# Attention and FFN layer: the value products of a group move from two sections of the PE program into one

## The reference, cut to what matters

```
n = layernorm(x)
q, k, v = n @ Wq, n @ Wk, n @ Wv        # 32 query heads, 8 key/value heads, 16 wide; rotary on q and k
att = q k^T / 4, causal                 # 4 query heads share one key/value head
ctx = softmax(att) @ v
x = x + ctx @ Wo
x = x + (silu(layernorm(x) @ Wg.T) * (layernorm(x) @ Wu.T)) @ Wd.T    # 1376 wide
```

## Time and profile before

| | |
|---|---|
| median of three runs | 810.72 us |
| the profiled execution's own time | 811.23 us |
| its span, from the first to the last instruction | 809.5 us |
| granted TensorE clock, mean over the span | 0.983 |
| busy: PE, DVE, ACT, POOL | 776.1, 432.7, 344.5, 210.3 us |

### The profile page before, as it was taken

One profiled execution on the slowest core, in us unless ns is written; L12 is line 12 of the kernel. 1 busy time (PEld: TensorE's weight loads), 2 busy tenths in 40 slices (PEclk: granted clock), 3 DMA queues, 4 the chain that ended last, 5 costly groups with the idle time before them and its releaser, 6 DMA issues.

```text
span 809.5 us, 12354 instructions
## 1 busy us (share of the span) xinstructions
PE 776.1 (96%) x4449; PEld 528.1 (65%) x4480; DVE 432.7 (53%) x744; ACT 344.5 (43%) x684; POOL 210.3 (26%) x382
## 2 busy tenths in 40 slices
PE   5789999999999999899799999999999999999998
PEld 4635555555555554354388887888878888788886
DVE  7686788687876777787345553223323243141112
ACT  3417768666777667667644232111112211121111
POOL 3406764467526863233400000000000000000000
PEclk9959999999999999999999999999999999999999
DMA  7436577234332336462168200512004120020001
GB/s 259 107 89 232 171 248 225 75 100 118 92 96 78 108 93 182 141 189 59 53 202 238 79 27 0 169 41 78 27 1 155 52 78 26 0 104 0 1 1 52
DMA packets 74613, 81.86 MB, mean 101 GB/s; under 512 B 8720, under 2 KB 58384, under 8 KB 74352
## 3 DMA queue, kind: packets, MB, share of 16 engines
q1 hardware_dynamic: 74128, 80.77, 32.8%
q10 hardware_dynamic: 432, 0.39, 0.2%
HBM read 57.02 MB, written 33.36 MB: 112 GB/s over the span
## 4 chain that ended last, share of the span: by engine, by line
PE 50%; DVE 0%; issue 0%; DVEq 0%
PE bank L1476 34%; PE ps_y L1528 15%; PE bank L1515 1%; DVE x_in L1458 0%; DVEq L1457 0%
## 5 line engine op out<-in xcount | busy, mean ns | idle before, releaser
L855 DVE TENSOR_REDUCE m_raw<-ps_s 128x1 f32<-128x512 f32 (+3 forms) x352 | 210.8, 634 | 65.7 <-PE ps_s L1099 63.1
L724 ACT ACTIVATE probs<-ps_t 128x512 f32<-128x512 f32 (+1 forms) x352 | 185.8, 563 | 101.8 <-PE ps_t L1126 100.6
L1433 DVE TENSOR_TENSOR h<-h,bank 128x512 f32<-128x512 f32 (+1 forms) x44 | 30.2, 687 | 216.8 <-PE bank L1476 216.1
L1096 PE MATMUL ps_s<-k_rows,q_rows 96*128 96x256 bf16 (+3 forms) x512 | 134.1, 315 | 7.1 <-DMA q_rows<-scratch_q_parts 4.6
L1126 PE MATMUL ps_t<-q_rows,k_rows 98*128 98x512 bf16 (+1 forms) x352 | 127.5, 367 | 6.5 <-DMA q_rows<-m_t 2.9
L1096 PEld LDWEIGHTS ps_s<-k_rows,q_rows 96*128 96x128 bf16 x512 | 44.2, 99 | 70.7 <-issue 30.5
L1371 ACT ACTIVATE h<-bank 128x512 f32<-128x512 f32 (+1 forms) x44 | 26.3, 599 | 149.1 <-PE bank L1476 149.1
L632 POOL TENSOR_SCALAR_AFFINE_SELECT probs<-probs 128x512 f32<-128x512 f32 x128 | 84.8, 662 | 0.0
L1139 PE MATMUL ps_o<-probs,v_ones 128*32 128x512 f32 (+3 forms) x1024 | 82.4, 440 | 0.3 <-ACT o_sb L734 0.3
L1377 ACT CAST h_hi<-h 128x512 fp32r<-128x512 f32 (+1 forms) x44 | 27.3, 620 | 127.1 <-DVE h L1433 127.1
L217 POOL TENSOR_TENSOR var_eps<-mean_var,eps 128x1 f32<-128x1 f32 x16 | 3.1, 191 | 289.9 <-DVE mean_var L212 289.9
(11 more groups left out here) (150 smaller groups left out, 1343.7 us busy)
## 6 DMA issues: line engine op xcount, KB each, us to landing
scratch_o<-o_sb SPq DMA_DIRECT2D x31, 256.0 KB, 2.3
q_rows<-scratch_q_parts SPq DMA_DIRECT2D x32, 192.0 KB
x_in<-in_x SPq DMA_DIRECT2D x16, 256.0 KB, 5.0
q_rows<-scratch_q_parts SPq DMA_DIRECT2D x32, 128.0 KB
x_res<-in_x SPq DMA_DIRECT2D x16, 256.0 KB, 2.7
o_in<-scratch_o SPq DMA_DIRECT2D x64, 64.0 KB
inverse<-scratch_inverse SPq DMA_DIRECT2D x64, 64.0 KB
out<-x_in SPq DMA_DIRECT2D x16, 256.0 KB, 2.1
```

The costliest lines, as they stand in the source:

```text
L724: nc.scalar.activation(probs[:, g % 2, heads * u:heads * (u + 1), CHUNK_AT[c]:CHUNK_AT[c + 1]], ps_t[:, pos % S_BANKS, 0:heads * CHUNK_N[c ...
L855: nc.vector.tensor_reduce(out=m_raw[:, g % 2, at:at + heads], op=ALU.max, axis=AXIS.X, in_=ps_s[:, (BANK_AT[i] + u) % S_BANKS, 0:heads * w ...
L1096: nc.tensor.matmul(bank[:, place], q_rows[r][0:ROWS, j, P * q:P * (q + 1)], k_rows[r][0:ROWS, 0:width], start=(place == 0), stop=False)
L1433: nc.vector.tensor_tensor(h[0:m, r], h[0:m, r], bank[units["up", f] % BANKS][0:m, :], ALU.mult).then_inc(h_ready, 1)
```

## The change

One entry of `PV_AT` now holds all four chunks, at (1, 1) of the next group, and the entry for (3, 3) is gone. After the last group, which has no next one, four chunks instead of two follow the loop. Nothing else is changed: no wait, no buffer, no DMA and no other engine's program.

```diff
-PV_AT = {(1, 1): (-1, (2, 3)), (3, 3): (0, (0, 1))}
+PV_AT = {(1, 1): (-1, (0, 1, 2, 3))}
 PV_EVACUATE = 2
...
                 if not has_next:
-                    for c in (2, 3):
+                    for c in range(TT):
                         weighted_v(b, NKV - 1, c)
```

## The result

| | before | after |
|---|---|---|
| median of five runs | 810.33 us (808.09 to 813.69) | 829.11 us (828.23 to 830.91) |
| the profiled execution's own time | 811.23 us | 830.91 us |
| its span | 809.5 us | 829.2 us |
| granted TensorE clock, mean | 0.983 | 0.977 |

The ratio is 1.0228, with a 95% interval from 1.0197 to 1.0259: **2.3% slower**, 18.8 us. The forecast was 823.0, from 811 to 830.

The account below looks back on a forecast made before the run. PE was taken to set the time of phase 1, DVE and ACT following with some slack. 811.2 - 6.2 + 12 + 6.5 = 823.5, and with the median 0.5 lower 823.0 us, range 811 to 830.

Parts of the forecast that it names:

- The clock's rival: Longer wait before group 25 brings a second half-clock stretch, 1.7 us, groups 30 and 31 as much again: 826.5; chance 0.09.
- the rival without a merging gain: Entering chunk 2 in the merged section costs a new entry, so the 6.2 us are not saved: 829 us; chance 0.05.
- Part 1: One section less in each of groups 0 to 30: 0.20 us saved on PE, 31 times, 6.2 us.
- Part 2: PE reaches (0, 0) 1.73 us earlier, DVE and ACT come late to a group's first banks: 12 us lost.
- the groups like 12: Groups where the rotated queries' splits end late; group 12 loses about 1.2 us, group 20 about 0.9.
- The POOL collision: A POOL operation stretches DVE's split of the maxima in group 12, 1.01 us against 0.18; 1.6 us taken off.
- the prediction's own sign: If groups without dense pieces or like group 11 are longer too, the forecast's mechanism is wrong.
- 11's pattern: In group 11 ACT is not late and DVE by 0.78 us, with 1.0 spare: nothing is lost.
- the fourth score bank needs the first reduce: At a group's start, this bank's need leaves DVE 1.0 us spare, so lateness below that costs nothing.
- Part 3: SP's staged rows and maxima come late at group starts, PE's way being 1.93 us shorter: 6.5 us lost.
- The rivals of the other side: DVE and ACT absorb their lateness, only DMA bites: 811.0, chance 0.14; or nothing is late, only the saving: 804.5, chance 0.09.

Follow-up runs that it names:

- experiments 2: Kernel after, with chunks 0 and 1 also multiplied a second time, for nothing, at (3, 3): 854.31 us, ratio 1.0567.
- experiments 3: Kernel after, with the merged section split: chunks 0 and 1 at (1, 0), chunks 2 and 3 at (1, 1) of the next group: 830.69 us, ratio 1.025.
- experiment 8: Kernel after, with batch 3's eight loads and the stores of the rotated rows issued behind the maxima's DMA on SP: 822.09 us, ratio 1.0167.
- experiment 1: Kernel before, with the section at (1, 1) in two, chunk 3 going to (1, 2): 817.0 us, ratio 1.0078.
- Experiment 9: Kernel after, with the three score banks used in turn across groups, without a restart at bank 0: 829.07 us, ratio 1.0202.
- experiment 5: Kernel after, with batch 3's eight loads issued one slot later on SP, behind the maxima's DMA: 824.36 us, ratio 1.0189.

## Why the prediction was right, and where it was not

**The sign and the mechanism held; the place within the range is partly luck.** It named DVE, ACT and SP, each late at a group's start once the section at (3, 3) is gone, and that is where the time went: experiments 2 and 3 show that the empty (3, 3) makes the loss, and experiment 8 parts the rows' share from the banks'. But 829.11 is 0.9 us inside the upper bound and 6.1 above the 823.0, and below, errors of 2 us cancel. The clock's rival, 826.5, was nearer, and 829, the number of the rival without a merging gain, is met for another reason.

**Part 1, one section less: 6.2 us, and it is 7.4.** The pieces of the earlier trace rows gave 0.20 a group, experiment 1 measured 0.24 and the kernel after shows 0.23. The rival without a merging gain is out.

**Part 2, DVE and ACT: the size held, the places half.** In the 22 groups without DMA or clock the sum was met (6.4 against 6.3) by luck, with two errors of over 2 us that cancel:
- In the groups like 12 the prediction had some 1.0, 0.8 and 0.7 us for 12, 4 and 20 (after the 0.20); they gave -0.12, 0.03 and 0.31. The POOL collision did not come back there, which the forecast had allowed 1.6 us for. The split of the maxima in group 12, for the 1.01 us of the earlier trace rows:

```profile
195.25 0.18 DVE L864 TENSOR_TENSOR m_parts<-m_raw,m_parts 128x16 bf16<-128x16 f32 x1 [0.59 <-ACT m_parts L705]
```

It moved instead, to groups 1, 9 and 17, where the split took 0.30, 0.24 and 0.24 us before and takes 1.02, 1.01 and 1.02 after. In group 9:

```profile
160.60 1.01 DVE L864 TENSOR_TENSOR m_parts<-m_raw,m_parts 128x16 bf16<-128x16 f32 x1 [1.14 <-ACT m_parts L705]
```

- In the groups that were to lose little or nothing (8, 16, 18, 21, 24: -0.20 to 0.0 each) it was 0.00 to 0.25. By the prediction's own sign, that its mechanism is wrong if the groups without dense pieces or with 11's pattern are longer too, this counts against it: 24, without such pieces, is 0.12 longer, and 3, 11 and 19 come to 0.03 only when SP's order is mended. The sign foretold 0.22 us between the product before (0, 0) and the next, and it is 0.38. The step that failed is "the fourth score bank needs the first reduce ... 1.0 us is spare". At a group's start the restart of the ring asks for more: the first two banks need the last two reduces. Experiment 9 shows that this slack is the tight one there, and that in its trace easing it alone mostly moves the wait.

**Part 3, the rows: right in the sum.** Forecast 6.5; PE's waits for rows and maxima grew by 4.3 + 1.1 = 5.4 us, and by 6.6 with the waits at the starts of groups 11 and 19 (0.65 and 0.53), which the profile puts down to ACT and DVE but SP's order took away. By places it was not met: 3, 7, 11 and 19 wait 0.53 to 0.69 us for 0.6 to 1.3 forecast, and 23, which the forecast didn't have, 0.69. Experiment 8 took most of it away by the order of SP's queue alone (1.1 + 1.5 us are left). The wait ahead of group 25 rose by 1.12 us (2.93 to 4.05) and not by 1.93. SP's chain in the kernel after:

```profile
323.01 0.36 SPq L443 DMA_DIRECT2D scratch_o<-o_sb  x1
...
333.43 0.72 SPq L437 DMA_DIRECT2D q_rows<-m_t  x1
```

It takes 10.4 us to the issue of the maxima, as before (10.5). PE was ready for them 11.24 us after the chain's start before and is after 9.86, so its way is 1.38 shorter and not 1.93: PE loses some 0.55 on it itself, which the forecast gave back in groups 3 to 11 but not here. The other 0.26 is that the maxima were there sooner after the chain's start, 13.91 us for 14.17. Group 5's wait was larger, 2.63 for 0.38 before and 0.9 forecast on top; it was 1.30 in experiments 3 and 5, so it differs between executions.

**The clock: the term that was mis-sized.** The sum had it at nothing, and a rival with 0.09 had 3.4 us of it, one more stretch after the wait ahead of group 25 and as much in groups 30 and 31. Measured are two more behind that wait, one more in 30 and 31, and one in group 5: four of 3.4 us. What one costs shows where a group has the same waits in two traces and the stretch in one of them only: group 31 1.83 with and 0.19 without (after and experiment 8), group 30 1.86 and 0.16 (after and 9). Group 7 has 2.77 in experiment 9 and 0.57 after, of which 0.6 is a longer wait for rows. That is 1.6 to 1.7 us each, as half of 3.4 us would be for a busy PE, some 6.5 for four, and the miss is 6.1. PE's busy time, 7.1 us more for the same instructions, says about the same. The rival was priced as an alternative to the forecast but was its consequence: a change that makes PE wait pays again for the wait in clock. The Trainium skill's warning on idle gaps in the middle of a kernel ("TensorE: Matmul & The Clock Gate", Why this matters for your kernels) was the better guide here than the single stretch of the earlier trace rows, though by the bound that it gives for such gaps only the wait of 4.05 us counts: the stretch behind 2.63 us and those in groups 30 and 31 it doesn't cover.

**The rivals of the other side** fell: the idle of DVE and ACT did not absorb the lateness, since after it PE waits for both more often.

## What to carry to other kernels

Work of the busiest engine that sits before a place where buffers are short is the others' time to catch up: before moving it, read the slack of each buffer at that place, over every wrap of its ring, and not the engine's idle in the whole. A wait added to TensorE is to be priced with the stretch at half clock that can follow it, which here cost 1.6 to 1.7 us for each 3.4 us. Merge sections of differently shaped products where the groups have slack for it, next to a product of their own shape, and leave the others alone: here that was worth 3 us in 13 groups, where merging in all cost 19.

## What was not expected of the hardware

**Half clock after the same wait has no fixed length.** The wait for group 25's maxima was 2.93 us before and 3.5 us at half clock followed; in experiment 1 it was 2.7, and 10.2 followed:

```profile
333.70:343.90 10.20, 9.97 (x53) 3.88 (x55) 8.52 (x16) 6.68 (x15) 2.54 (x8) 0.50 0.32 97
```

PE's rows fill 9.97 of these 10.2 us, so the profile shows next to no idle of PE within the stretch. After 1.4 us of wait there were 6.8 us in experiment 5, 3.4 in 8 (1.5 us) and none in 2. What decides between them is open; no experiment was made on it.

**A wait that PE doesn't show.** The 0.16 and 0.08 us ahead of (0, 0) and (0, 1) are in no PE row and in no sum of PE's waits, only in the distances of the products' starts and in PEld's waits. Over the 29 group starts with scores these distances are 15.8 us beyond 0.22 each, and 5.9 of them, the part that the modelled end of 0.38 covers, is missing from the list of PE's waits.
